# Two-layer graph kernel on one core: h transposed by VectorE blocks and a DRAM scratch in place of TensorE

## The chip, the cores and the metric

The kernel runs on one core of a Trainium2 chip. The metric is the device time of one execution in microseconds (us); lower is better. Engines: PE is TensorE (matrix products), DVE is VectorE, ACT is ScalarE, POOL is GpSimd, SP is SyncE, which here only issues DMAs. Each engine works through its own instructions in order and waits on semaphores.

## The reference, cut to what matters

128 graphs of 128 nodes with 512 features, one adjacency matrix for all, all in fp32:

```python
h = jnp.maximum(_layernorm(x, axis=-1), 0.0)
# layer 0, all products over d, e, m
z_l, z_g, v = h @ W_lang.T, h @ W_grav.T, h @ W_V.T
zn  = z_l / jnp.maximum(norm(z_l), EPS)
A_l = jnp.maximum(zn @ zn.T, 0) * not_eye * adj
A_g = jnp.exp(-squared_distances(z_g) / (2 * sigma * sigma)) * not_eye * adj
K   = w_l * A_l / rowsum(A_l) + (1 - w_l) * A_g / rowsum(A_g)
x   = x + (K @ v) @ W_O.T
h   = jnp.maximum(_layernorm(x, axis=-1), 0.0)
# layer 1: W = adj * adj
x   = x + einsum('bnf,nm->bmf', h, W) + bias
```

## The kernel before, in words

The 128 graphs are worked in 32 groups (NG) of 4 (GB). A semaphore counts everything that is handed on; nothing is planned at run time, the order on each engine is written out by hand in a function `iteration(i)` per engine (PE line 858, ACT line 381, DVE line 644, POOL line 312, SP line 216). Groups 2 to 30 run as a loop, the others are unrolled. A matrix product in fp32 precision is made of three products of fp32r halves: every operand is split into a `hi` part (written by ACT, from PSUM) and a `lo` part (the difference, written by DVE, line 529 for all products from PSUM).

A group i goes through these stages on PE, in this order:

- Y stage: 8 blocks of 3, 6, 9 or 12 products (`y_block`, a over 4, l over 2; 60 products of 512 columns), from the transposed h (`hT`) and weights folded in the setup. ACT writes `y_hi` (line 388), DVE `y_lo` (line 529). Between block 6 and 7 stand 4 transposes of K of the group before (line 837).
- K v stage: 12 products for the group before (`k_v`), whose result DVE adds to x (`residual`, lines 596 and 600: x2 and its statistics).
- P stage: 48 products of 256 columns into `p_ps`; ACT copies them out in two halves (line 410).
- V stage: per graph 12 products of hT with MT (`v_done`), then 4 transposes of h of the NEXT group (`transposes_h`, line 819), 128x128 each, into the same ring of four PSUM banks. ACT writes `v_hi` (line 422) and `hT_hi` (line 378), DVE `v_lo` and `hT_lo` (line 529). After graph 2 stand 8 transposes of P (line 897), which wait for `p_shifted` (ACT line 456).
- Layer 1 stage: 12 products for the group before (`layer1`), from `h2` hi and lo; DVE adds them to x_out (line 642), and SP stores x_out.

A use of a ring bank waits until DVE has drained the use four before it (`free`, line 811). So the first Y block of a group waits for the first x_out of the stage before.

What the change touches besides: the statistics of x of the next group stand on DVE inside the Y stage (`x_stats`, line 541, 4 instructions around `kt_lo`, line 586); POOL makes factors of them (`norm1`, lines 264 to 278), ACT applies them after the Y stage (`apply_norm1`, line 373: h). For layer 1, POOL makes factors of the statistics of x2 (`norm2`, the same lines 264 to 278), ACT writes `h2f` with them (`h2_full`, line 444), ACT copies `h2_hi` (line 451), POOL takes `h2_lo` (line 295). POOL also adds the bias (line 288) and multiplies out the diagonal of P (line 302), of which DVE takes row sums (lines 693, 695) for the shift on ACT (line 456). DVE adds P and its transpose (`sum_s`, line 708), ACT takes the exponential (line 461).

SP per group: load of x of group i+2 (line 200, 1 MB), the row norms out to DRAM and back spread over all partitions (lines 212 and 214), four stores of 256 KB (line 206).

Of the kernel before, what the change touches and what calls it, by code (L numbers as in the profile page):

```python
# [5 lines left out]
ALU = mybir.AluOpType  # L25
# [5 lines left out]
P = 128  # L31
GB = 4
# [6 lines left out]
def gnn_pair(nc, x, adj, w_lang, w_grav, w_v, w_o, gate_logit, log_sigma, bias, out):  # L39
# [9 lines left out]
    blk = {ac: n for n, ac in enumerate(TRI)}  # L49

# [4 lines left out]
    PER = G_USES + GB + 2 * GB + GB  # L55
# [4 lines left out]

    HI_PER = G_USES + 2 * GB

# [6 lines left out]
    with ExitStack() as ctx:  # L69
# [48 lines left out]

        raw_l = x2[:, :, :]
# [10 lines left out]

        rn_dram = nc.dram_tensor("rn_dram", [P, GB], F32).ap()
# [45 lines left out]
        h2_split_dve = sem("h2_split_dve")  # L177
        ln2_last = sem("ln2_last")
# [10 lines left out]
        def wait_for(eng, sem, count):  # L189

            if not isinstance(count, int) or count > 0:
                eng.wait_ge(sem, count)

# [4 lines left out]
        def _(sp):  # L198
# [16 lines left out]

            def iteration(i, load=True, store=True, after=True):
                if load:
# [8 lines left out]
                if store:  # L226
                    store_out(i - 1, first_use(i) + PER - GB * (1 if after else 2))

# [15 lines left out]
            store_out(NG - 1, first_use(NG))  # L244
# [116 lines left out]
        def _(act):  # L361
# [14 lines left out]
            def t_hi(g, b, n):  # L376
                act.wait_ge(t_done, GB * g + b + 1)
                act.activation(hT[0][:, :, b], bank(n).rearrange("p (c m) -> p c m", c=C), ACT.Copy)\
                   .then_inc(hi_ready, 1)

            def iteration(i, before=True, after=True):
# [3 lines left out]
                for a in range(C):  # L385
                    for l in range(2):
# [16 lines left out]
                if after:  # L403
                    apply_norm1(i + 1)
# [13 lines left out]
                for b in range(GB):  # L418
# [5 lines left out]
                    if after:  # L424
                        t_hi(i + 1, b, n)
                        n += 1
# [10 lines left out]
            def h2_full(g, b, last=False):  # L437
# [65 lines left out]
            apply_norm1(0, wait_free=False)  # L503
            lw_hi(1, side, side_hi)
            for b in range(GB):
                t_hi(0, b, SETUP + b)
# [15 lines left out]
        def _(dve):  # L522
# [11 lines left out]
            def x_stats(g, b0, b1):  # L534
# [109 lines left out]
            def iteration(i, before=True, after=True):  # L644
# [36 lines left out]
                for b in range(GB):  # L681
                    hi = hi + 1
                    lo(v[1][:, b], bank(n), v[0][:, b], hi).then_inc(drained, 1)
                    n += 1
                    hi = hi + 1
# [10 lines left out]
                    if b == 2:  # L696
                        sum_s(i)
                if before:
# [95 lines left out]

            iteration(0, before=False)
            iteration(1)
            with dve.Fori(2, NG - 1) as i:
                iteration(i)
            iteration(NG - 1, after=False)
            g = NG - 1  # L800
            residual(g, 0, first_use(g) + PER - GB, last=True)
# [8 lines left out]
        def _(pe):  # L810
# [4 lines left out]
            def transposes_h(g, b, n, use):  # L815
# [153 lines left out]
```

## Time and profile before

| | |
|---|---|
| median of 3 runs | 1308.2 us (1307.92 to 1308.43) |
| span of the profiled execution, first to last instruction | 1305.4 us |
| median of the runs less that span | 2.8 us |
| PE busy | 1281.8 us, 98% |
| DVE busy | 924.4 us, 71% |
| ACT busy | 708.3 us, 54% |
| POOL busy | 610.3 us, 47% |
| mean granted TensorE clock | 0.997 of full speed |
| DMA | 80.02 MB, 61 GB/s over the span |

The profile is of one execution. No time of its own around its span is reported for it, so the runs' median stands for it; the two differ by 2.8 us, launch and end. Busy time counts instructions at work; PE's matmuls are pipelined, so they overlap in the records and a busy PE can still wait a little.

### The profile page before, as it was taken

The numbers are of one execution on the slowest core, as the hardware profiler recorded it, in microseconds if no ns is written. First come the engines' busy times: TensorE is split into PE (matmuls) and PEld (weight loads), VectorE is DVE, ScalarE is ACT, GpSimd is POOL, SyncE is SP. The second block draws the span as 40 slices with busy tenths as digits, with TensorE's granted clock in tenths as the row PEclk, the third lists the DMA queues.
The fourth block names the chain that finished last, engine by engine and source line by source line (L and its number), as shares of the span: only waits on it lengthen the run. The fifth ranks groups of instructions, "written<-read, shape, count | busy, mean of one in ns | idle before, by whom it ended". The sixth has DMA issues, their size and how long they took to land.

```text
span 1305.4 us, 22778 instructions
## 1 busy us (share of the span) xinstructions
PE 1281.8 (98%) x6820; PEld 1094.9 (84%) x6820; DVE 924.4 (71%) x1609; ACT 708.3 (54%) x1324; POOL 610.3 (47%) x995
## 2 busy tenths in 40 slices
PE   7999999999999999999999999999999999999995
PEld 6888888888888888888888888888888888888884
DVE  5477666777666777666778666778666778666678
ACT  5445655545655545655545655545555555555534
POOL 1124555444555444455444455444455444455534
PEclk9999999999999999999999999999999999999998
DMA  5011221111221121221121221121221121221011
GB/s 204 33 31 51 73 70 43 64 68 45 72 72 40 64 72 40 72 72 40 64 72 40 72 72 40 64 72 40 72 72 41 64 71 40 72 72 51 22 41 65
DMA packets 47006, 80.02 MB, mean 61 GB/s; under 512 B 7952, under 2 KB 8080, under 8 KB 46992
## 3 DMA queue, kind: packets, MB, share of 16 engines
q1 hardware_dynamic: 46416, 79.51, 18.3%
q10 hardware_dynamic: 576, 0.33, 0.1%
q8 instruction: 8, 0.13, 0.0%
q14 instruction: 6, 0.05, 0.0%
HBM read 46.20 MB, written 33.62 MB: 61 GB/s over the span
## 4 chain that ended last, share of the span: by engine, by line
PE 95%; DVE 3%; ACT 1%; DMA 1%; issue 0%; POOL 0%; SPq 0%; DVEq 0%
PE ring L824 74%; PE p_ps L824 14%; PE ring L819 4%; PE p_ps L897 2%; PE kt_ps L837 1%; DMA h2f<-in_L_gnn_W_grav 1%; DVE x_out L642 0%; DVE hT_lo L529 0%; ACT h L373 0%; DVE bn L600 0%; DVE y_lo L746 0%; DVE x L596 0%; DVE bn L541 0%; DVE K L580 0%; DVE Lw_lo L761 0%
## 5 line engine op out<-in xcount | busy, mean ns | idle before, releaser
L529 DVE TENSOR_TENSOR v_lo<-ring,v_hi 128x512 fp32r<-128x512 f32 x128 | 88.5, 692 | 290.2 <-ACT v_hi L422 290.2
L388 ACT ACTIVATE y_hi<-ring 128x512 fp32r<-128x512 f32 x256 | 149.0, 594 | 253.1 <-PE ring L824 250.6
L264 POOL TENSOR_TENSOR ln<-bn 128x4 f32<-128x4 f32 x63 | 13.1, 208 | 546.2 <-DVE bn L541 533.1
L824 PE MATMUL ring<-hT_hi,Lw_hi 128*128 128x512 f32 x640 | 252.5, 395 | 3.1 <-DVE hT_lo L529 3.1
L824 PE MATMUL ring<-hT_hi,Lw_lo 128*128 128x512 f32 x640 | 249.7, 390 | 0.0
L824 PE MATMUL ring<-hT_lo,Lw_hi 128*128 128x512 f32 x640 | 249.1, 389 | 0.0
L824 PE MATMUL ring<-MT_hi,hT_hi 128*128 128x512 f32 x512 | 208.7, 408 | 0.0
L824 PE MATMUL ring<-MT_hi,hT_lo 128*128 128x512 f32 x512 | 201.0, 393 | 0.0
L824 PE MATMUL ring<-MT_lo,hT_hi 128*128 128x512 f32 x512 | 200.3, 391 | 0.0
L295 POOL TENSOR_TENSOR h_lo<-h2f,h_hi 128x512 fp32r<-128x512 f32 x124 | 157.9, 1295 | 57.8 <-ACT h_hi L451 57.8
L529 DVE TENSOR_TENSOR y_lo<-ring,y_hi 128x512 fp32r<-128x512 f32 x256 | 170.1, 685 | 13.2 <-ACT y_hi L388 12.8
L288 POOL TENSOR_TENSOR x_out<-x,bias_sb 128x512 f32<-128x512 f32 x128 | 163.4, 1299 | 21.4 <-DVE bn L600 19.6
L824 PE MATMUL p_ps<-y_hi,hT_lo 128*128 128x256 f32 x512 | 144.9, 283 | 0.0
L824 PE MATMUL p_ps<-y_lo,hT_hi 128*128 128x256 f32 x512 | 144.9, 283 | 0.0
L824 PE MATMUL p_ps<-y_hi,hT_hi 128*128 128x256 f32 x512 | 144.7, 283 | 0.0
L824 PEld LDWEIGHTS ring<-hT_hi,Lw_hi 128*128 128x128 f32 x640 | 120.2, 188 | 27.6 <-issue 1.9
L373 ACT ACTIVATE h<-x_ring,ln 128x512 f32 (+1 forms) x128 | 94.0, 807 | 87.9 <-POOL ln L278 87.9
L824 PEld LDWEIGHTS ring<-hT_hi,Lw_lo 128*128 128x128 f32 x640 | 120.1, 188 | 25.7
L824 PEld LDWEIGHTS ring<-hT_lo,Lw_hi 128*128 128x128 f32 x640 | 120.3, 188 | 24.2
L824 PEld LDWEIGHTS ring<-MT_hi,hT_lo 128*128 128x128 f32 x512 | 96.1, 188 | 21.5
L824 PEld LDWEIGHTS ring<-MT_lo,hT_hi 128*128 128x128 f32 x512 | 96.7, 189 | 16.5
L824 PEld LDWEIGHTS ring<-MT_hi,hT_hi 128*128 128x128 f32 x512 | 96.5, 188 | 16.3
(160 smaller groups left out, 2586.0 us busy)
## 6 DMA issues: line engine op xcount, KB each, us to landing
x_ring<-in_x SPq DMA_DIRECT2D x32, 1024.0 KB, 5.3
out<-x_out SPq DMA_DIRECT2D x128, 256.0 KB, 2.1
rn_cols<-rn_dram SPq DMA_DIRECT2D x31, 256.0 KB, 3.6
x<-in_L_gnn_W_lang SPq DMA_DIRECT2D x4, 256.0 KB, 5.5
h2f<-in_L_gnn_W_grav SPq DMA_DIRECT2D x1, 1024.0 KB, 8.9
chain<-in_L_gnn_W_O SPq DMA_DIRECT2D x1, 1024.0 KB, 12.8
x_ring<-in_L_gnn_W_V SPq DMA_DIRECT2D x1, 1024.0 KB, 14.6
rn_dram<-rn SPq DMA_DIRECT2D x31, 2.0 KB, 1.4
```

What stands on the lines that cost most here:

```text
L264: pool.tensor_tensor(t[:, SUM], bn[:, :, 1], bn[:, :, 4], ALU.add).then_inc(step, 1)
L288: pool.tensor_tensor(x_out[:, b], x2[:, b], bias_sb[:, :], ALU.add).then_inc(x2b_ready, 1)
L295: pool.tensor_tensor(h2[1][:, b], h2f[:, b], h2[0][:, b].bitcast(F32), ALU.subtract)\
L373: act.activation(h[:, b], xb, ACT.Relu, bias=ln1[:, SHIFT, b:b + 1], scale=ln1[:, RSTD, b:b + 1]).then_inc(h_ready, 1)
L388: act.activation(y[0][:, a, :, l], bank(n).rearrange("p (b m) -> p b m", b=GB), ACT.Copy)\
L529: return dve.tensor_tensor(out, ps, part(hi), ALU.subtract)
L819: mm = pe.transpose(bank(n)[:, c * P:(c + 1) * P], h[:, b, c * P:(c + 1) * P], ident[:, :])
L824: mm = pe.matmul(out, lhsT, rhs, start=(k == 0), stop=(k == len(terms) - 1))
L837: mm = pe.transpose(kt_ps[:, b], K[:, b], ident[:, :])
L897: mm = pe.transpose(p_ps[:, k // 2, k % 2], P_sb[:, k // 2, k % 2], ident[:, :])
```

## The change

h of the next group is no longer transposed by PE. ACT normalizes h during the last two Y blocks; DVE transposes it in 32x32 blocks (4 instructions of 128x512), into the memory of `h2f`; one DMA writes these blocks to a DRAM scratch (1 MB), four DMAs of 256 KB read them back, each into 32 partitions, so that the blocks land in the rows of the full transpose (`h_turned`); ACT and DVE split `hT` from there instead of from PSUM. Because `h2f` holds the blocks until they are out, `h2_full` waits for `turned`. The statistics of x move to the V stage of the group before. The ring of banks has 4 uses less per group.

```diff
@@ SP
+            def turn_h(g):
+                sp.wait_ge(blocks_ready, GB * g)
+                sp.dma_start(blocks_dram, h_blocks).then_inc(blocks_stored, 16)
+                sp.wait_ge(blocks_stored, 16 * g)
+                for j in range(NQ):
+                    sp.dma_start(h_turned[j * Q:(j + 1) * Q], blocks_dram[:, j].rearrange("(i p) e -> p i e", p=Q))\
+                      .then_inc(turned, 16)
+
             def iteration(i, load=True, store=True, after=True):
+                if after:
+                    turn_h(i + 1)
                 if load:
...
@@ ACT
-            def apply_norm1(g, wait_free=True):
-                act.wait_ge(ln1_step, LN_STEPS * (g + 1))
-                if wait_free:
-                    act.wait_ge(t_done, GB * g)
-                for b in range(GB):
+            def normalize(g, b0):
+                if b0 == 0:
+                    act.wait_ge(ln1_step, LN_STEPS * (g + 1))
...
+                for b in range(b0, b0 + GB // 2):
...
+            def turned_hi(g, b):
+                if b == 0:
+                    act.wait_ge(turned, TURN * g)
+                act.wait_ge(v_done, GB * (g - 1) + b + 1)
+                act.activation(hT_columns(0, b), h_columns(b), ACT.Copy).then_inc(ht_hi, 1)
...
+                        if after and G_USES - 2 <= n < G_USES:
+                            normalize(i + 1, (n - G_USES + 2) * GB // 2)
...
-                if after:
-                    apply_norm1(i + 1)
...
                     if after:
-                        t_hi(i + 1, b, n)
-                        n += 1
+                        turned_hi(i + 1, b)
...
@@ def h2_full
                 if b == 0:
                     wait_for(act, h2_split, GB * g)
+                    act.wait_ge(turned, TURN * (min(g + 2, NG - 1) if isinstance(g, int) else g + 2))
@@ DVE
+            def turn_blocks(g, b):
+                if b == 0 and not (isinstance(g, int) and g < 3):
+                    dve.wait_ge(h2_split, GB * (g - 2))
+                dve.wait_ge(h_ready, GB * g + b + 1)
+                out = h_blocks.rearrange("p j (c b q) -> p c b j q", c=C, b=GB)[:, :, b]
+                dve.transpose(out, h[:, b].rearrange("p (c j q) -> p c j q", c=C, j=NQ)).then_inc(blocks_ready, 1)
+
+            def turned_lo(g, b):
+                dve.wait_ge(ht_hi, GB * (g - 1) + b + 1)
+                dve.tensor_tensor(hT_columns(1, b), h_columns(b), part(hT_columns(0, b)), ALU.subtract)\
+                   .then_inc(ht_lo, 1)
...
-                        if n == G_USES - 2:
-                            if before and after:
-                                x_stats(i + 1, 0, GB // 2)
-                            if before:
-                                kt_lo(i - 1)
-                            if before and after:
-                                x_stats(i + 1, GB // 2, GB)
-                        if not before and n == G_USES:
-                            x_stats(i + 1, 0, GB)
+                        if after and n >= G_USES - 1:
+                            turn_blocks(i + 1, 2 * (n - G_USES + 1))
+                        if before and n == G_USES - 1:
+                            kt_lo(i - 1)
+                        if after and n >= G_USES - 1:
+                            turn_blocks(i + 1, 2 * (n - G_USES + 1) + 1)
...
-                    t_lo(b, n, hi).then_inc(drained, 1 if before or b < GB - 1 else 1 + GB)
-                    n += 1
+                    turned_lo(i + 1, b)
...
                     if b == 2:
                         sum_s(i)
+                    if stats and b >= 2:
+                        x_stats(i + 2, (b - 2) * GB // 2, (b - 1) * GB // 2)
@@ PE, iteration
+                wait_for(pe, ht_lo, GB * i)
...
-                    if after:
-                        transposes_h(i + 1, b, n, use + n)
-                        n += 1
```

Group 0's h is still transposed by PE, in the setup.

## Rows read from the trace of the kernel before

**Rows 1.** Head of the page: busy time per engine.
```profile
PE 1281.8 (98%) x6820; PEld 1094.9 (84%) x6820; DVE 924.4 (71%) x1609; ACT 708.3 (54%) x1324; POOL 610.3 (47%) x995
```

**Rows 2.** Chain that ended last, one group: start us, duration us, what.
```profile
568.53 0.44 PE ring L819 x4
568.97 2.76 PE ring L824 x12
...
579.45 13.65 PE ring L824 x60
...
604.78 2.75 PE ring L824 x12
...
618.45 13.65 PE ring L824 x60
```

**Rows 3.** Timeline of DVE, same group: start, duration, line, operation, count.
```profile
596.98 0.69 DVE L529 TENSOR_TENSOR y_lo<-ring,y_hi 128x512 fp32r<-128x512 f32 x1 [0.21 <-ACT y_hi L388]
597.59 1.28 DVE L596 TENSOR_TENSOR x<-ring,x_ring 128x512 f32<-128x512 f32 x2
601.16 1.28 DVE L600 BATCH_NORM_STATS2 bn<-x 128x6 f32<-128x512 f32 x2
618.68 0.69 DVE L529 TENSOR_TENSOR v_lo<-ring,v_hi 128x512 fp32r<-128x512 f32 x1 [0.94 <-ACT v_hi L422]
619.88 1.88 DVE L642 TENSOR_TENSOR x_out<-ring,x_out 128x512 f32<-128x512 f32 x3
```

**Rows 4.** Timeline of ACT, same group.
```profile
605.78 1.52 ACT L444 ACTIVATE h2f<-x,ln 128x512 f32<-128x512 f32 x2 [0.37 <-POOL ln L278]
607.57 0.60 ACT L422 ACTIVATE v_hi<-ring 128x512 fp32r<-128x512 f32 x1 [0.26 <-PE ring L824]
611.84 0.58 ACT L422 ACTIVATE v_hi<-ring 128x512 fp32r<-128x512 f32 x1
612.79 1.14 ACT L451 ACTIVATE h_hi<-h2f 128x512 fp32r<-128x512 f32 x2
```

**Rows 5.** The page's costliest groups: instructions that the change adds, by their nearest kind.
```profile
L541 DVE BATCH_NORM_STATS2 bn<-x_ring 128x6 f32 x116 | 74.1, 681 | 0.0
L550 DVE TENSOR_TENSOR chain<-chain,rn_cols 128x512 f32<-128x512 f32 x31 | 33.1, 1068 | 0.0
L708 DVE TENSOR_TENSOR chain<-p_ps,chain 128x1024 f32<-128x1024 f32 x32 | 38.9, 1215 | 0.0
```

**Rows 6.** The page's DMA issues: KB each, median us to landing.
```profile
x_ring<-in_x SPq DMA_DIRECT2D x32, 1024.0 KB, 5.3
out<-x_out SPq DMA_DIRECT2D x128, 256.0 KB, 2.1
```

**Rows 7.** Load of x alone, window 600 to 610 us in 40 slices: GB/s.
```profile
GB/s 0 0 0 0 0 0 0 0 0 0 98 147 41 131 229 156 385 393 434 410 426 401 410 336 156 33 8 0 0 0 0 0 0 0 0 0 0 0 0 0
```

**Rows 8.** Start of the kernel: SP issues four loads of 256 KB; ACT starts on each.
```profile
0.81 1.81 SPq L231 DMA_DIRECT2D x<-in_L_gnn_W_lang  x4
...
4.82 0.63 ACT L477 ACTIVATE y_hi<-x 128x512 fp32r<-128x512 f32 x1 [0.85 <-DMA x<-in_L_gnn_W_lang]
...
8.62 0.63 ACT L477 ACTIVATE y_hi<-x 128x512 fp32r<-128x512 f32 x1 [0.57 <-DMA x<-in_L_gnn_W_lang]
```

**Rows 9.** Last group: DVE beside POOL at work.
```profile
1278.33 1.14 DVE L568 TENSOR_TENSOR deg<-deg,rn 128x8 f32<-128x8 f32 x1
1298.53 1.47 DVE L637 TENSOR_TENSOR h_lo<-h2f,h_hi 128x512 fp32r<-128x512 f32 x1
1276.76 2.69 POOL L295 TENSOR_TENSOR h_lo<-h2f,h_hi 128x512 fp32r<-128x512 f32 x2 [2.82 <-ACT h_hi L451]
1296.93 2.52 POOL L288 TENSOR_TENSOR x_out<-x,bias_sb 128x512 f32<-128x512 f32 x2
```

**Rows 10.** SP's issues in the same group.
```profile
601.56 0.41 SPq L200 DMA_DIRECT2D x_ring<-in_x  x1
613.38 0.33 SPq L214 DMA_DIRECT2D rn_cols<-rn_dram  x1
```

More of the change, by code:

```diff
@@ L31 @@
 P = 128
+Q = 32
 GB = 4
@@ L49, in gnn_pair @@
     blk = {ac: n for n, ac in enumerate(TRI)}
+    NQ = P // Q
+    TURN = 16 * NQ
+    assert C == NQ
     G_USES = 2 * C
     SETUP = C
-    PER = G_USES + GB + 2 * GB + GB
+    PER = G_USES + GB + GB + GB
     def first_use(i):
         return SETUP + GB + PER * i
-    HI_PER = G_USES + 2 * GB
+    HI_PER = G_USES + GB
     def first_hi(i):
@@ L116, in gnn_pair @@
         deg = sb("deg", [P, 4, GB, 2])
+        h_turned = sb("h_turned", [P, NQ, C * GB * Q])
+        h_blocks = h2f[:, :, :].rearrange("p b d -> p (b d)").rearrange("p (j e) -> p j e", j=NQ)
         raw_l = x2[:, :, :]
@@ L177, in gnn_pair @@
         h2_split_dve = sem("h2_split_dve")
+        blocks_ready, blocks_stored, turned = sem("blocks_ready"), sem("blocks_stored"), sem("turned")
+        ht_hi, ht_lo = sem("ht_hi"), sem("ht_lo")
         ln2_last = sem("ln2_last")
@@ L192, in wait_for, with h_columns, hT_columns @@
                 eng.wait_ge(sem, count)
+        def h_columns(b):
+            return h_turned[:, :, :].rearrange("p i (c b q) -> p c b i q", c=C, b=GB)[:, :, b]
+        def hT_columns(part, b):
+            return hT[part][:, :, b].rearrange("p c (i q) -> p c i q", q=Q)
         block = ctx.enter_context(nc.Block())
@@ L226, in iteration @@
                 if store:
-                    store_out(i - 1, first_use(i) + PER - GB * (1 if after else 2))
+                    store_out(i - 1, first_use(i) + PER - GB)
             w_rows = w_lang.rearrange("(c p) n -> p c n", p=P)
@@ L365, in _ @@
             act.dma_start(bias_sb[:, :], bias.unsqueeze(0).to_broadcast([P, D])).then_inc(consts_loaded, 16)
-            def apply_norm1(g, wait_free=True):
-                act.wait_ge(ln1_step, LN_STEPS * (g + 1))
-                if wait_free:
-                    act.wait_ge(t_done, GB * g)
-                for b in range(GB):
+            def normalize(g, b0):
+                if b0 == 0:
+                    act.wait_ge(ln1_step, LN_STEPS * (g + 1))
+                    if isinstance(g, int) and g == 1:
+                        act.wait_ge(t_done, GB)
+                    elif not isinstance(g, int) or g > 1:
+                        act.wait_ge(blocks_ready, GB * (g - 1))
+                for b in range(b0, b0 + GB // 2):
                     xb = x_ring[:, bass.ds(g % SLOTS, 1), b].rearrange("p s d -> p (s d)")
@@ L502, in _ @@
             act.activation(sig, lsig, ACT.Exp).then_inc(exp_gate, 1)
-            apply_norm1(0, wait_free=False)
+            normalize(0, 0)
+            normalize(0, GB // 2)
             lw_hi(1, side, side_hi)
             for b in range(GB):
-                t_hi(0, b, SETUP + b)
+                t_hi(b, SETUP + b)
             act.wait_ge(a2_step, 1)
@@ L642, in output, with iteration @@
                 dve.tensor_tensor(x_out[:, b], bank(n), x_out[:, b], ALU.add).then_inc(drained, 1)
-            def iteration(i, before=True, after=True):
+            def iteration(i, before=True, after=True, stats=True):
                 n = 0
@@ L682, in iteration @@
                     hi = hi + 1
-                    lo(v[1][:, b], bank(n), v[0][:, b], hi).then_inc(drained, 1)
+                    lo(v[1][:, b], bank(n), v[0][:, b], hi)\
+                        .then_inc(drained, 1 if before or b < GB - 1 else 1 + GB)
                     n += 1
-                    hi = hi + 1
-                    t_lo(b, n, hi).then_inc(drained, 1 if before or b < GB - 1 else 1 + GB)
-                    n += 1
+                    turned_lo(i + 1, b)
                     if b == 0:
@@ L793, in _ @@
             dve.tensor_tensor(A2[1][:, :], adj2[:, :], part(A2[0][:, :]), ALU.subtract).then_inc(a2_step, 1)
+            x_stats(1, 0, GB)
             iteration(0, before=False)
             iteration(1)
-            with dve.Fori(2, NG - 1) as i:
+            with dve.Fori(2, NG - 2) as i:
                 iteration(i)
+            iteration(NG - 2, stats=False)
             iteration(NG - 1, after=False)
             g = NG - 1
-            residual(g, 0, first_use(g) + PER - GB, last=True)
+            residual(g, 0, first_use(NG), last=True)
             h2_lo(g, 0)
@@ L813, in free, with transposes_h @@
                 wait_for(pe, drained, use - BANKS + 1)
-            def transposes_h(g, b, n, use):
-                pe.wait_ge(h_ready, GB * g + b + 1)
+            def transposes_h(b, n, use):
+                pe.wait_ge(h_ready, b + 1)
                 free(use)
@@ L922, in _ @@
             for b in range(GB):
[L923 removed]
+                transposes_h(b, SETUP + b, SETUP + b)
             pe.wait_ge(w_loaded["o"], 16)
@@ L938, in _ @@
             g = NG - 1
-            use = first_use(g) + PER - GB
+            use = first_use(NG)
             pe.wait_ge(kt_split, NG)
```

8 lines of the change are left out of this document (4 added, 4 removed).

## The prediction

> **What bounds the kernel now.** I read the head of the page first: PE is busy 98% of the span, the next engine, DVE, 71% [rows 1]. Then the chain that ended last, around one group in the middle: it runs on PE alone, stage behind stage, with no wait between [rows 2]. Its long pieces of 13.65 us (12 products of layer 1, then 48 of the next Y stage) start at 579.45 and 618.45, so a group takes 39.00 us, and 30 of them are alike. 12 of 60 products into that piece, at 618.45 + 2.7 = 621.1, the next Y stage starts. Last I read the timelines of DVE, ACT and SP over the same group [rows 3, 4, 10], to see how far behind PE they run. Here the cover is thin. The first Y block needs the bank that the first x_out frees; that x_out starts at 619.88 and ends at 620.56 [rows 3], only 0.5 us ahead of 621.1. ACT starts h2f 0.37 us after POOL's factors are there, and v_hi 0.26 us after PE's result [rows 4]. So PE bounds, but one queue of dependences (x2 statistics, POOL's factors, h2f, v_hi, v_lo, x_out) is under a microsecond from bounding too.
>
> **The change, part by part.**
>
> 1. PE loses the transposes of h: 4 x 0.44 us per group [rows 2], 1.76 us, in 31 groups 55 us. This is a gain only as long as PE sets the end.
>
> 2. DVE gets 4 block transposes of 128x512 per group. The trace has none. The nearest row is bn_stats over 128x512 from SBUF at 0.68 us [rows 5]; in a row such instructions start 0.60 apart (two take 1.28 us [rows 3]). Above it I bound by the slowest 128x512 there is, 1.07 us, which reads with a stride [rows 5]; below by nothing, since a gain is excluded. I take 0.60, because one pass over 512 elements costs the same in all other DVE rows. The four x statistics leave this place, so DVE's work in the Y stage is the same, but its place is not: the statistics stood ahead of the last y_lo, and DVE even waited 0.21 us for ACT there [rows 3]. Transposes 2 and 3 stand behind it, since ACT normalizes them only in block 7, and so ahead of the residual: this starts at 597.59 + 1.2 = 598.8 in place of 597.59. x2's statistics, norm2 and h2f follow 1.2 us later: 605.78 becomes 607.0.
>
> 3. The way through DRAM. The last blocks are ready at 597.59 + 2 x 0.60 + 0.08 = 598.9. SP's queue is clear: it has stored the group before and waits here (the load of x started at 601.56 [rows 10] and now goes behind the turn; its data is wanted only some 10 us later; the row norms come later still and have slack too). Out: 1 MB to DRAM. A store of 256 KB lands in 2.1 us [rows 6]; the 0.79 MB more, at the load's full pace of about 0.4 MB per us [rows 7], cost 2.0: 4.1 us. The upper bound is x's load of 1 MB, 5.3 [rows 6]. I take 4.1, as the direction is that of the store. Back: four DMAs of 256 KB, issued in a row. Lower bound: the single load of 1 MB, about 5.4 us. Upper: at half its pace. Its data take 1.05 MB / 0.4 = 2.6 us at full pace [rows 7], so half adds 2.6: 8.0. Between stands the nearest row in form, four loads of 256 KB issued one behind the other: from 0.81 to 8.62, 7.8 us, landing after the first about 1.3 us apart [rows 8] (in the start-up of the kernel, beside small loads). I take 7.8. The blocks are back at 598.9 + 4.1 + 7.8 = 610.8.
>
> Each quarter writes only 32 partitions. The Trainium skill (SBUF — State Buffer, Door 1: The DMA port swizzle) says that a transfer into partitions 0 to 31 or 0 to 63 reaches 8 of 16 ports and so about half the bandwidth, and that issuing two such transfers doesn't help. No row here has such a transfer. By that rule the way back takes the 8.0 above and the total is 6 us higher; by the row of x's load it takes 5.4, the second rival.
>
> 4. The new wait on ACT. h2f waits for `turned`: 610.8, not 605.78, nor the 607.0 of part 2. Queued behind it on ACT are v_hi, hT_hi, the rest of h2f, the shift, h2_hi. From h2f to v_hi of graph 1 ACT takes 611.84 - 605.78 = 6.06, less the 0.26 wait: 5.80; from there to v_hi of graph 2 it takes 2.05 (h2_hi starts at 612.79 and takes 1.14 [rows 4]). So v_hi 2 starts at 618.65 and ends at 619.25. On the way PE waits: its transposes of P need the shift, done at 616.6, while PE, without the transposes of h, comes there at 604.78 + 3 x 2.76 = 613.1 [rows 2]. That stall of 3.5 us is not extra; it lies beside the same path.
>
> 5. DVE behind v_hi 2, all in order: v_lo 0.60, hT_lo 0.60, the sum with P transposed 1.2 [rows 5], two x statistics 1.2, v_lo 0.60, hT_lo 0.60, two x statistics 1.2, x_out 0.68. Together 6.68. The x statistics are the 2.4 us that the change moves here; before, x_out came straight behind hT_lo. x_out ends at 625.95.
>
> 6. A collision. hT_lo read PSUM and SBUF; now it reads SBUF twice. In the last group, DVE instructions that read SBUF twice stretch where POOL is at work: a 128x8 one takes 1.14 us, ending as POOL's h_lo does, and h_lo on DVE takes 1.47 in place of 0.68, by what POOL's bias addition had left [rows 9]. POOL's h_lo of 4 x 1.26 us starts at 618.3 in the new order, so hT_lo 2 at 619.9 falls into the second of them, ending at 620.8: 0.8 us. Bounds: nothing, and twice 1.26. The Trainium skill (SBUF — State Buffer, SBUF: two separate sides) calls this port pair an exclusive lock against a DVE instruction with two SBUF inputs; by that rule the 0.8 stands, and without it, the total is 24 us lower.
>
> **Sum.** x_out ends at 626.75, 5.65 us after the 621.1 at which the Y stage starts now: a group takes 44.65 us. 30 groups (1 to 30) have the wait: 30 x 5.65 = 169.5. Group 0 has no h2f, its blocks are back long before the V stage: 1 us less. Group 30 has no x statistics: some 2 us less. Span 1305.4 + 169.5 - 3 = 1471.9; with the 2.8 us by which the runs' median lies over the span, 1474.7.
>
> **Rivals.**
>
> *A, full pace on the way back.* The quarters stream like one load: 5.4 us. Then h2f starts at 608.4, a group costs 3.25 more, 30 x 3.25 - 3 + 1308.2 = 1403 us. For it: the same packets of 2 KB; against: rows 8 and four separate issues. 20%.
>
> *B, the way through DRAM is covered.* It decides where the round trip is under 607.0 - 598.9 = 8.1 us; then only parts 2, 5 and 6 are left: 5.65 - 3.8 = 1.85 per group, 1361 us; without the collision 1337. Against it: a store and a load of 1 MB alone take 4.1 + 5.4 = 9.5. 6%.
>
> *C, PE goes on setting the end: faster.* If x_out still ends ahead of PE, all of part 1 is gained: 31 x 1.76 = 55, 1254 us. The place is x_out behind DVE's queue in the V stage. It decides if h2f starts no later than about 605, that is if the turn's wait never ends last, and DVE's statistics run in its gaps. For it: DVE is idle for several us in every V stage, and PE is the only engine over 71% [rows 1]. Against it: those gaps lie before v_hi 0, not behind v_hi 2, where 6.68 us stand in a row. 8%.
>
> *D, everything at its upper end.* Out 5.3, back 8.0, DVE transposes 1.07 (0.8 more), a second collision: 8 to 8.5 us per group, about 1550 us. 6%.
>
> That the change does nothing is no case: 1.8 us of PE work and a round trip per group cannot vanish together by chance; 1% for no change, where gain and wait balance. That PE gets slower by clock is not one either: it was granted full speed throughout and is still busy over 80%.
>
> **How the numbers follow.** Forecast, 59%: 1475 us. Its own spread, by collision and start-up share of rows 8, is 1440 to 1510. To leave out no more than 2 in 10, the range goes down through rival A to 1385 and up part of the way to D, 1520; B, C and the end of D are left out. Slower by over 0.2% (about what a measurement of this kernel can tell from no change) are the forecast, A, B and D: 91%. Within 0.2%: 1%. Faster: C, 8%.
>
> **What the profile of after would show.** Right: a period of 44 to 45 us; PE busy near 84%, with idle time before the transposes of P and before the first Y block; ACT's largest wait in the middle groups at h2f, ended by the DMA into h_turned; out in about 4 us, back in about 8; a DVE transpose of 0.7 us; hT_lo with a mean over 0.68. Wrong: the chain still on PE alone (C); ACT's h2f ended by POOL's factors (B); quarters that land in under 4 us each with a return under 6 in all (A); or the chain going through POOL or the load of x, which no part here expects.

## The result, and the profile after

The changed kernel takes 1467.2 us (median of 4 runs, 1465.9 to 1468.2) against 1308.1 us before: ratio 1.1218, 95% interval 1.1202 to 1.1234, so 159 us slower, inside the range and 8 us under the forecast. The profiled execution took 1465.9 us with a span of 1464.2. One execution further below, of the kernel with no trip, ran at a mean clock of 0.557, took 2063 us and is left out.

Head of the page of the changed kernel, its chain by engine and line, and its DMA issues (KB each, median us to landing):

```profile
PE 1269.1 (87%) x6324; PEld 1043.1 (71%) x6324; DVE 1020.8 (70%) x1733; ACT 701.8 (48%) x1324; POOL 651.9 (45%) x995
...
PE 38%; DMA 19%; DVE 16%; ACT 11%; issue 11%; SPq 2%; DVEq 1%; ACTq 0%; POOL 0%
...
x_ring<-in_x SPq DMA_DIRECT2D x32, 1024.0 KB, 7.8
...
blocks_dram<-h2f SPq DMA_DIRECT2D x31, 1024.0 KB, 3.9
h_turned<-blocks_dram SPq DMA_DIRECT2D x124, 256.0 KB, 5.1
```

[rows 1] showed PE at 98%. Now PE is at 87% with 496 instructions less, and the chain, PE alone around the group of [rows 2], is more than half on others, 19% of it on the two transfers. Three views of one group show it in order of time. The timeline of SP (start, duration, line, what):

```profile
623.34 0.33 SPq L215 DMA_DIRECT2D blocks_dram<-h2f  x1
627.22 1.75 SPq L218 DMA_DIRECT2D h_turned<-blocks_dram  x4
629.46 0.42 SPq L197 DMA_DIRECT2D x_ring<-in_x  x1
...
667.69 0.33 SPq L215 DMA_DIRECT2D blocks_dram<-h2f  x1
```

The timelines of ACT and, below it, DVE, for the same group; they answer to [rows 3, 4]:

```profile
634.74 1.52 ACT L460 ACTIVATE h2f<-x,ln 128x512 f32<-128x512 f32 x2 [4.90 <-DMA h_turned<-blocks_dram]
...
642.45 0.58 ACT L438 ACTIVATE v_hi<-ring 128x512 fp32r<-128x512 f32 x1
```

```profile
622.01 1.29 DVE L565 STREAM_TRANSPOSE h2f<-h 128x512 f32<-128x512 f32 x2
...
643.68 1.59 DVE L569 TENSOR_TENSOR hT_lo<-h_turned,hT_hi 128x512 fp32r<-128x512 f32 x1
645.19 1.21 DVE L734 TENSOR_TENSOR chain<-p_ps,chain 128x1024 f32<-128x1024 f32 x1
646.33 1.27 DVE L558 BATCH_NORM_STATS2 bn<-x_ring 128x6 f32 x2
647.52 0.67 DVE L546 TENSOR_TENSOR v_lo<-ring,v_hi 128x512 fp32r<-128x512 f32 x1
648.11 0.67 DVE L569 TENSOR_TENSOR hT_lo<-h_turned,hT_hi 128x512 fp32r<-128x512 f32 x1
648.71 1.27 DVE L558 BATCH_NORM_STATS2 bn<-x_ring 128x6 f32 x2
649.91 1.86 DVE L671 TENSOR_TENSOR x_out<-ring,x_out 128x512 f32<-128x512 f32 x3
```

POOL's h_lo, beside which the hT_lo of 1.59 us runs:

```profile
642.11 5.55 POOL L302 TENSOR_TENSOR h_lo<-h2f,h_hi 128x512 fp32r<-128x512 f32 x4 [1.34 <-ACT h_hi L467]
```

How to read them together: the blocks leave at 623.34 and are in DRAM at 627.22 (the return is issued then); ACT starts h2f at 634.74, 7.5 us later, after 4.90 us of waiting for the DMA; v_hi of graph 2 ends at 643.03; from there DVE works without a gap to x_out. PE's timeline shows what all this holds up, the first products of the transposes of P, of layer 1 (twice) and of the next Y stage, with the waits before them:

```profile
640.56 1.09 PE L925 MATMUL p_ps<-ident,chain 128*128 128x128 f32 x8 [3.17 <-ACT chain L472]
...
646.55 0.49 PE L852 MATMUL ring<-h_hi,A_hi 128*128 128x512 f32 x1 [0.74 <-POOL h_lo L302]
...
648.24 0.50 PE L852 MATMUL ring<-h_hi,A_hi 128*128 128x512 f32 x1 [0.74 <-DVE v_lo L546]
...
650.63 0.50 PE L852 MATMUL ring<-hT_hi,Lw_hi 128*128 128x512 f32 x1 [1.42 <-DVE x_out L671]
```

The period, from one issue of the blocks to the next, is 667.69 - 623.34 = 44.35 us, where it was 39.00. From here on "period" is read in this way, from SP's timeline.

### The profile page after: what moved, and what is told of

Same layout as the page of the kernel before. It is cut to its first block, busy times and chain, and to the rows that moved or that the text cites. A ratio compares the mean times of both kernels' runs of the same rounds, so it can differ in the third digit from the quotient of the medians.

```text
span 1464.2 us, 21983 instructions
## 1 busy us (share of the span) xinstructions
PE 1269.1 (87%) x6324; PEld 1043.1 (71%) x6324; DVE 1020.8 (70%) x1733; ACT 701.8 (48%) x1324; POOL 651.9 (45%) x995
## 4 chain that ended last, share of the span: by engine, by line
PE 38%; DMA 19%; DVE 16%; ACT 11%; issue 11%; SPq 2%; DVEq 1%; ACTq 0%; POOL 0%
PE ring L852 35%; DMA h_turned<-blocks_dram 11%; DMA blocks_dram<-h2f 7%; DVE bn L558 5%; ACT v_hi L438 3%; DVE sq L717 3%; SPq L218 2%; DVE hT_lo L569 2%; PE p_ps L852 2%; ACT h_hi L467 2%; ACT chain L472 2%; ACT h2f L460 2%; DVE h2f L565 2%; DVE x_out L671 1%; DVE chain L734 1%
## 5 line engine op out<-in xcount | busy, mean ns | idle before, releaser
L852 PE MATMUL ring<-hT_hi,Lw_hi 128*128 128x512 f32 x640 | 257.1, 402 | 43.5 <-DVE x_out L671 40.1
L302 POOL TENSOR_TENSOR h_lo<-h2f,h_hi 128x512 fp32r<-128x512 f32 x124 | 171.8, 1414 | 45.3 <-ACT h_hi L467 45.3
L460 ACT ACTIVATE h2f<-x,ln 128x512 f32<-128x512 f32 x128 | 97.2, 805 | 156.2 <-DMA h_turned<-blocks_dram 147.2
L426 ACT ACTIVATE chain<-p_ps 128x512 f32<-128x512 f32 x64 | 38.3, 598 | 230.2 <-PE p_ps L852 230.2
L925 PE MATMUL p_ps<-ident,chain 128*128 128x128 f32 x256 | 38.4, 298 | 96.0 <-ACT chain L472 96.0
```

What stands on the lines that cost most here:

```text
L302: pool.tensor_tensor(h2[1][:, b], h2f[:, b], h2[0][:, b].bitcast(F32), ALU.subtract)\
L426: act.activation(P_sb[:, 2 * half:2 * half + 2], p_ps[:, 2 * half:2 * half + 2], ACT.Copy)\
L852: mm = pe.matmul(out, lhsT, rhs, start=(k == 0), stop=(k == len(terms) - 1))
L925: mm = pe.transpose(p_ps[:, k // 2, k % 2], P_sb[:, k // 2, k % 2], ident[:, :])
```

## The experiments

The forecast was right in time. But each of its terms could be wrong with another making up for it, so I took them apart one by one: the x statistics behind v_hi (2.4 us), h2f's wait for the blocks (3.8 us), and the form of the trip. The collision of hT_lo with POOL was not taken out by itself. A second question came up on the way: can the change be made to pay?

**x statistics out of the tail.**

```diff
-                    if stats and b >= 2:
-                        x_stats(i + 2, (b - 2) * GB // 2, (b - 1) * GB // 2)
+                    if stats and b < 2:
+                        x_stats(i + 2, b * GB // 2, (b + 1) * GB // 2)
```

> The changed kernel with the statistics of x in the V stage behind graphs 0 and 1 in place of graphs 2 and 3. My theory: v_lo of graph 2 to the first x_out is a row of DVE instructions that sets the end, and the 2.4 us of statistics stand in it. In front of it DVE idles 1.62 and 0.76 us behind graphs 0 and 1, so the first pair costs nothing and the second about 0.4: 2.0 us less per group, 44.35 becomes 42.4, the total 1467 - 60 = 1407 us. Rival, that only the wait for the way through DRAM decides: DVE's work behind it would be covered by PE, no change, 1467 us.

Measured: 1415.6 us, 52 less, where the expectation had 60. Period 42.6 us (43.4 in two groups): 1.8 of the 2.4 us come out. The rival (no change) is refuted: the statistics are a term of their own, and most of it was real. The mean clock is 0.968 here in place of 0.986. The windows show its falls to half around the transposes of P (at 662 to 668 us and the like), where PE has slack: groups with a fall of some 3 us take as long as groups without one, and in the two groups of 43.4 us it lasts some 7 us.

**The same statistics late in the kernel before**, which says whether they cost by themselves:

```diff
                         if n == G_USES - 2:
-                            if before and after:
-                                x_stats(i + 1, 0, GB // 2)
                             if before:
                                 kt_lo(i - 1)
-                            if before and after:
-                                x_stats(i + 1, GB // 2, GB)
...
                     if b == 2:
                         sum_s(i)
+                    if stats and b >= 2:
+                        x_stats(i + 2, (b - 2) * GB // 2, (b - 1) * GB // 2)
```

> The kernel before, with nothing changed but the place of the statistics of x: in the V stage behind graphs 2 and 3, as the change has them. My theory: DVE has 0.94 us free ahead of v_lo 3, the rest of the 2.4 us stands ahead of the first x_out, which then ends 1.46 us later, at 622.0 in place of 620.56, 0.9 behind PE: 30 x 0.9 = 27, 1335 us. Rival, that PE covers it: 1308 us.

Measured: 1339.1 us, ratio 1.0237 (1.0220 to 1.0254), period 40.1 us; the theory had 1335. So 1.1 of the 2.4 us end behind PE even with no transposes, no trip and no new wait: the cover of 0.5 us between x_out and the Y block that the prediction read in [rows 3] was as thin as it looked.

**Blocks in memory of their own**, so that h2f need not wait (diag and A are free at that time):

```diff
-        h_blocks = h2f[:, :, :]...
+        h_blocks = chain[:, 1:3]...
...
             def diagonal(g):
+                pool.wait_ge(blocks_stored, 16 * (g + 1))
...
-                    act.wait_ge(turned, ...)
...
             def turn_blocks(g, b):
-                    dve.wait_ge(h2_split, GB * (g - 2))
+                    dve.wait_ge(k_ready, g - 1)
...
```

> The changed kernel with the 32x32 blocks in the memory of diag and A (free at that time) in place of h2f's, so that h2f does not wait for the blocks' return; hT_hi of graph 0 still does, and ACT stands there. My theory: h2f starts 3.3 us earlier, at POOL's factors, but hT_hi 0 waits where it stood 2 us later before; what follows on ACT moves up by 2.0 us: 42.4 us per group, 1407 us. Rival, that the shared buffer is the whole price of the wait: 3.3 us per group, 1367 us.

Measured: 1466.8 us. A miss by 60 us: no gain at all. The timeline of ACT shows that the edit did what it should: h2f starts behind POOL's factors, 8.05 us after the blocks were issued (at 625.62) in place of 11.40, and it is hT_hi that waits for the DMA, until 11.42 us after the issue; in the changed kernel it stood at 13.31. So ACT gains the 2 us that were foreseen.

```profile
633.67 1.52 ACT L460 ACTIVATE h2f<-x,ln 128x512 f32<-128x512 f32 x2 [1.54 <-POOL ln L285]
635.10 0.58 ACT L439 ACTIVATE v_hi<-ring 128x512 fp32r<-128x512 f32 x1
637.04 0.63 ACT L396 ACTIVATE hT_hi<-h_turned 128x512 fp32r<-128x512 f32 x1 [1.37 <-DMA h_turned<-blocks_dram]
```

Of the timelines of POOL and DVE in the same group, one line each:

```profile
636.04 2.54 POOL L295 TENSOR_TENSOR x_out<-x,bias_sb 128x512 f32<-128x512 f32 x2
...
637.71 1.43 DVE L569 TENSOR_TENSOR hT_lo<-h_turned,hT_hi 128x512 fp32r<-128x512 f32 x1 [1.31 <-ACT hT_hi L396]
```

Two things took the gain. hT_lo 0 now runs beside POOL's bias addition and takes 1.43 us in place of 0.68. And the clock, which the windows of 2 us at the start of the Y stage show (busy time per engine and number of instructions, then granted clock, DMA share, GB/s):

```profile
648.00:650.00 2.00, 1.25 (x6) 0.61 (x4) 2.00 (x5) 0.23 (x1) 0.72 (x1) 1.00 0.00 0
650.00:652.00 2.00, 0.58 (x3) 0.31 (x2) 2.00 (x4) 0.00 (x0) 0.72 (x4) 0.82 0.00 0
652.00:654.00 2.00, 2.00 (x6) 1.52 (x6) 2.00 (x4) 0.60 (x1) 1.76 (x5) 0.50 0.68 253
654.00:656.00 2.00, 2.00 (x9) 1.65 (x8) 2.00 (x4) 0.60 (x1) 1.22 (x2) 0.83 0.65 245
```

The granted clock goes from full (2.4 GHz) to half (1.2 GHz) for some 3 us, and the products of the next Y stage come 0.43 us apart in place of 0.23. PE had idled 1.95 us before the transposes of P and 0.73, 0.75 and 1.42 us shortly before the fall. The fall comes in most groups, not in all: the periods are 44.4 to 44.7, and every eighth is 43.1. So a fall costs 1.5 us, and without it the edit would be worth 1.2 us per group.

**The same with PE kept busy.** 14 products whose results nobody uses, on operands that lie ready, stand where PE would idle; nothing else differs.

```diff
+                        if before and after:
+                            filler(6)
                         pe.wait_ge(p_shifted, i + 1)
...
+                        if after and b >= 2:
+                            filler(2)
                         layer1(i - 1, b, n + b, use + n + b)
+                    if after:
+                        filler(4)
```

> The run with own blocks, and on PE 14 products per group (128x512, one pass each, result used by nobody) put in front of its waits: 6 before the transposes of P, 2 before each of the last two products of layer 1, 4 before the Y stage. In the run with own blocks the first 6 products of the Y stage ran at 0.43 us each in place of 0.23, the granted clock 0.50 there. My theory: the clock fell because PE had stood still before; filled, it stays at 1.00, the Y stage gets 1.3 us back and so do the blocks: 43.1 us per group, 1428 us. Rival, that the fall has another reason or costs nothing on the path: 1467 us or more.

Measured: 1428.9 us, mean clock 0.998 in place of 0.954, and a period of 43.0 to 43.2 in every group but the first. That is the time foreseen. It shows that the 38 us were the clock's, and that PE's idleness brought its fall about. The Trainium skill (TensorE: Matmul & The Clock Gate, Why this matters for your kernels) warns of idle gaps between bursts of products. Here no gap before the fall was longer than 1.95 us, while the changed kernel, with one of 3.17 us at the same place, shows no fall in the group above.

**The form of the way back.** First one DMA of 1 MB into 128 partitions in place of four quarters:

```diff
-                for j in range(NQ):
-                    sp.dma_start(h_turned[j * Q:(j + 1) * Q], blocks_dram[:, j]...)
+                sp.dma_start(h_turned[:, :, :], blocks_dram).then_inc(turned, 16)
```

> The changed kernel with the return in one DMA of 1 MB into all 128 partitions in place of four of 256 KB into 32 each; the same bytes, but the blocks are not put in their places, so h of later groups is not transposed as a whole. My theory (32 partitions at a time take it to half pace): the return takes 5.4 us as x's load of before in place of 7.4, so 2.0 less per group, 1407 us. Rival, the time lies in reading what was just written to DRAM: 7.4 us again, 1467 us.

Then four DMAs of 256 KB again, each into 128 partitions:

```diff
-                    sp.dma_start(h_turned[j * Q:(j + 1) * Q], blocks_dram[:, j]...)
+                    sp.dma_start(h_turned[:, j], blocks_dram[:, j]).then_inc(turned, 16)
```

> As the run with one return, but in four DMAs of 256 KB, each into all 128 partitions (one quarter of the columns each); the same bytes and packets of 2 KB, the blocks again not put in their places. It parts the number of issues from the number of partitions. My theory: partitions decide, and this run is within 0.5 us per group of the one return: 5.4 to 5.9 us, 1407 to 1422 us. Rival, four issues in a row decide: 7.4 us as in the changed kernel, 1467 us.

Measured: 1413.5 us for the single return (1407 foreseen) and 1469.0 us for the four wide ones, where the theory had 1407 to 1422 and the rival 1467. On its time alone the second would be the rival's; the traces say otherwise. The DMA issues of the two pages (one return; four wide ones):

```profile
h_turned<-blocks_dram SPq DMA_DIRECT2D x31, 1024.0 KB, 4.8
```

```profile
h_turned<-blocks_dram SPq DMA_DIRECT2D x124, 256.0 KB, 3.7
```

A quarter lands in 5.1 us when it goes to 32 partitions and in 3.7 when it goes to 128. So the form of the destination costs 1.4 to 1.7 us of the way back (h2f waits 3.2 us on average in place of 4.9: 96 in place of 147 us over 30 groups), and four issues in a row of 0.4 us each cost another 1.0 against a single one, with which h2f waits 2.2. This agrees with the Trainium skill (SBUF — State Buffer, Door 1) in direction; half the pace, as the prediction estimated it, would have made it 2.6 us. But the time of the four wide returns did not fall: their mean clock is 0.960, the windows show a fall at the start of the Y stage in every group but the first, and the periods are 44.3 to 44.6 from the third group on. If the fall costs the 1.5 us that it costs above, an estimate, they would be 42.9 without it. The single return alternates. Its issues of the blocks, three periods:

```profile
562.41 0.33 SPq L215 DMA_DIRECT2D blocks_dram<-h2f  x1
...
604.23 0.33 SPq L215 DMA_DIRECT2D blocks_dram<-h2f  x1
...
646.04 0.33 SPq L215 DMA_DIRECT2D blocks_dram<-h2f  x1
...
689.40 0.33 SPq L215 DMA_DIRECT2D blocks_dram<-h2f  x1
```

41.8, 41.8 and 43.4 us: over the whole run 41.8 and 43.3 for the most part turn about, and the 13 groups of 43.3 are those in which the clock falls.

**No trip at all.** DVE writes the blocks straight into `h_turned`; no DMA, no wait for one.

```diff
-                if after:
-                    turn_h(i + 1)
...
-h_blocks = h2f...
+h_blocks = h_turned[:, :, :]
```

> The changed kernel without the way through DRAM: VectorE transposes its 32x32 blocks straight into h_turned and both DMA steps are left out, so h of later groups is turned in blocks only. Everything else stays, the late statistics and the shifted residual too. My theory: h2f starts at POOL's factors, 3.35 us earlier; hT_lo of graph 0 then meets POOL's bias addition (0.75 us, as in the run with own blocks) and, if PE's clock falls as it did there, 1.3 us go as well. 44.35 - 3.35 + 0.75 = 41.75 us per group, 1389 us; with the clock's fall 43.05, 1428 us. Rival, that the way through DRAM is the whole loss: 1308 us or less, since PE has 1.76 us less to do per group.

Measured: 1410.8 us, in one execution. The theory had 1389 without a fall of the clock and 1428 with one in every group; the rival (1308 or less) is refuted. The periods are 41.8 and 43.3 for the most part turn about, the same as with a single return, and again the 13 groups of 43.3 are those with a fall, some 20 us in all. That is the bound behind the trip: with the trip gone, the kernel still takes 103 us more than before. The timeline of DVE in one group:

```profile
654.21 1.49 DVE L564 TENSOR_TENSOR hT_lo<-h_turned,hT_hi 128x512 fp32r<-128x512 f32 x1
...
661.30 1.60 DVE L564 TENSOR_TENSOR hT_lo<-h_turned,hT_hi 128x512 fp32r<-128x512 f32 x1
...
663.96 1.27 DVE L555 BATCH_NORM_STATS2 bn<-x_ring 128x6 f32 x2
...
666.34 1.27 DVE L555 BATCH_NORM_STATS2 bn<-x_ring 128x6 f32 x2
```

Two collisions of 0.8 and 0.9 us, the 2.4 us of statistics, and h2f 1.2 us late behind transposes 2 and 3: these are matters of order, not of the trip. That they can be put right is for the next kernels to show.

**The order put right.** If the cost lies in places, the change can be kept and the places mended. The first attempt: own blocks, `h_turned` on the memory of h, four slots of x with the load one group earlier, the x statistics behind the residual, where DVE waits for v_hi, and the copies out of the turned h put off by one or two graphs.

```diff
-    SLOTS = 3
+    SLOTS = 4
...
                 n += GB
+                if after and stats:
+                    x_stats(i + 2, 0, GB)
...
-                    turned_lo(i + 1, b)
+                    if b == 1:
+                        turned_lo(i + 1, 0)
+                        turned_lo(i + 1, 1)
+                    if b == 3:
+                        turned_lo(i + 1, 3)
...
                         sum_s(i)
+                        turned_lo(i + 1, 2)
...
```

> The whole change in another order, complete: blocks in the memory of diag and A; h_turned in the memory of h, which frees the room for a fourth slot of x; so x is loaded a group earlier and its statistics stand in DVE's long gap behind the residual; hT_hi and hT_lo of graphs 0 and 1 come behind h2_hi 0 and 1, the others behind. The blocks land 28.4 us into the group and are wanted at about 30.6, so nothing waits for them. My theory: the queue behind v_hi 2 is v_lo, sum, hT_lo, v_lo, hT_lo, x_out, and the first x_out ends at 37.5 to 38.4 us into the group, against PE's 37.2: 38.2 us per group, 30 x 0.8 less than before, 1284 us. Rival: collisions of hT_lo with POOL's h_lo (up to 1.26 each, three of them) and a fall of PE's clock (1.3) eat this: 39.5 to 41 us per group, 1325 to 1370 us.

Measured: 1342.7 us (1339.4 to 1344.7), 58 above the theory; the rival was right. Period 39.7 us, and 41.3 in the seven groups in which the clock falls, some 11 us in all. Timeline of DVE in the V stage:

```profile
625.44 1.03 DVE L733 TENSOR_SCALAR sqc<-sq 128x4 f32<-128x4 f32 x1
...
628.79 2.57 DVE L577 TENSOR_TENSOR hT_lo<-h,hT_hi 128x512 fp32r<-128x512 f32 x2 [0.87 <-ACT hT_hi L399]
...
633.01 1.30 DVE L577 TENSOR_TENSOR hT_lo<-h,hT_hi 128x512 fp32r<-128x512 f32 x1
```

Alone these take 0.17, 1.28 and 0.68 us: 2.8 us lost beside POOL. And h2f still comes late: it waits 1.6 us for POOL's factors. With these durations I wrote the queues of the five engines out as a timetable (for each instruction its pitch, what it waits for, and a lock between DVE instructions with two SBUF inputs and POOL's large ones) and tried the places of the copies in it. The best order has normalization after the fourth and sixth y copy, all transposes after the sixth y, the first two copies ahead of the shift:

```diff
+                        if after and n in (4, 6):
+                            normalize(i + 1, (n - 4) * GB // 4)
...
+                        if n == G_USES - 2:
+                            if after:
+                                turn_blocks(i + 1, 0)
+                                turn_blocks(i + 1, 1)
+                            if before:
+                                kt_lo(i - 1)
+                            if after:
+                                turn_blocks(i + 1, 2)
+                                turn_blocks(i + 1, 3)
...
+                    if after and b == 0:
+                        turned_hi(i + 1, 0)
+                        turned_hi(i + 1, 1)
                         shift(i, 1)
...
+                        turned_lo(i + 1, 0)
+                        turned_lo(i + 1, 1)
                     if b == 2:
                         sum_s(i)
+                        turned_lo(i + 1, 3)
...
```

> The re-ordered change once more, with every step of the turned h moved a few microseconds earlier: ScalarE normalizes the next group's h behind the fourth and the sixth y product instead of the sixth and the seventh, VectorE turns all four blocks behind the sixth y and before the last two (they stood behind the seventh and eighth), hT_hi 0 and 1 come in the slot of graph 0 before the shift, hT_lo 0 and 1 behind sqc, and hT_lo 3 behind the sum. In the run before this one the period was 39.7 us with collisions of VectorE's subtractions with GpSimd's additions (hT_lo 0 and 1 2.57 us for two, hT_lo 2 1.30, sqc 1.03 in place of 0.17). My theory: the cost of the change is a matter of order alone, the 11.3 us of the DRAM trip is covered when the blocks leave at the sixth y, and the 1.76 us of transposes that TensorE is rid of show at last: my timetable of the queues gives 38.1 us per group where it gives 38.9 for the kernel before (measured 39.0), so 1308.1 less 30 x 0.8 = 1284 us, 1275 to 1300. Rival: VectorE and GpSimd meet wherever the copies are put, because VectorE's third of the group is full: then the collisions cost what TensorE gains, and the time is 1305 to 1345. Second rival: the four normalizations ahead of the last y copies hold the y banks back, TensorE waits in the Y stage, its granted clock falls under 0.98 and the time lies over 1345.

Measured: **1282.1 us** (1281.0 to 1282.9), ratio 0.9805 (0.9788 to 0.9821), the fastest of all: 26 us under the kernel before. The head of the page, the chain by engine, and SP's issues of two groups:

```profile
PE 1234.4 (96%) x6324; PEld 1045.0 (82%) x6324; DVE 1032.7 (81%) x1733; ACT 708.9 (55%) x1324; POOL 671.8 (53%) x995
...
PE 74%; DVE 12%; ACT 7%; issue 6%; DMA 1%; ACTq 0%; POOL 0%; DVEq 0%; SPq 0%
```

```profile
624.33 0.33 SPq L215 DMA_DIRECT2D blocks_dram<-chain  x1
628.22 1.75 SPq L218 DMA_DIRECT2D h<-blocks_dram  x4
...
662.35 0.33 SPq L215 DMA_DIRECT2D blocks_dram<-chain  x1
```

The period is 38.0 to 38.1 us in every group but the first (38.02 here; the timetable said 38.1), the trip takes as long as ever (3.9 us out), and no engine waits for it: DMA is 1% of the chain. PE gets 0.98 of its 1.76 us; 0.65 of the rest is a wait for x_out before the last product of layer 1:

```profile
647.37 0.49 PE L866 MATMUL ring<-h_hi,A_hi 128*128 128x512 f32 x1 [0.65 <-DVE x_out L678]
```

Order alone could hardly have brought the kernel before there: its PE is busy 40.00 of 40 us in the middle of the run. That was not tried.

**Which part of the order it was.** Two kernels, each the 1282.1 us one with one thing put back. In the first, normalization and transposes stand where the change has them:

```diff
-                        if after and n in (4, 6):
-                            normalize(i + 1, (n - 4) * GB // 4)
+                        if after and G_USES - 2 <= n < G_USES:
+                            normalize(i + 1, (n - G_USES + 2) * GB // 2)
...
-                        if n == G_USES - 2:
-                            if after:
-                                turn_blocks(i + 1, 0)
...
+                        if after and n >= G_USES - 1:
+                            turn_blocks(i + 1, 2 * (n - G_USES + 1))
...
```

> The kernel of 1282.1 us with one thing put back: normalization and block transposes stand where the change has them (behind the sixth and seventh y copy and the seventh and eighth y), so that the blocks leave later; the x statistics, the memories and the places of the copies out of the turned h stay. My theory: the trip through DRAM is then uncovered by the time by which the blocks leave later (about 1.2 us); my timetable gives 39.3 us per group against 38.1, so 1282 + 30 x 1.2 = 1318 us, 1300 to 1335. Rival: the places of the copies alone made the gain over the 1342.7 us of the first re-ordered kernel, and 1.2 us of lateness are swallowed by the slack before the first hT_hi: 1280 to 1295.

Measured: 1296.3 us (1294.4 to 1297.0), period 38.5 to 38.7. That lies between the ranges of the theory (1300 to 1335) and the rival (1280 to 1295), nearer to the rival, and the timetable's 39.3 us was a miss: the trip stays covered, and no engine waits for it. What is lost is h2f again, behind the residual that stands behind transposes 2 and 3. Its waits in the two kernels, in this one and in the 1282.1 us one:

```profile
ACT h2f L467 <- POOL ln L288: 46.4, 30, 1.6
```

```profile
ACT h2f L467 <- POOL ln L288: 10.9, 30, 0.4
```

1.2 us per group. So of the 61 us between the two re-ordered kernels 46 belong to the places of the copies (some 11 of them by the falls of the clock, which this kernel does not have) and 14 to the earlier blocks.

In the second, the x statistics are back in the V stage:

```diff
-                if after and stats:
-                    x_stats(i + 2, 0, GB)
...
+                    if stats and b >= 2:
+                        x_stats(i + 2, (b - 2) * GB // 2, (b - 1) * GB // 2)
```

> The kernel of 1282.1 us with one other thing put back: the four bn_stats on the next x stand behind the v_lo of graphs 2 and 3, as the change has them, and not behind the residual, where VectorE waits 3.4 us for v_hi anyway. My theory: they stand between the last v_lo and x_out, for which TensorE waits, so their 2.4 us come out nearly whole unless VectorE waits there: my timetable gives 39.8 us per group against 38.1, so 1282 + 30 x 1.8 = 1335 us, 1320 to 1350, in line with the 51.7 us that the same move gave back in the changed kernel. Rival: VectorE has 0.7 and 0.8 us of waiting before the v_lo of graphs 1 and 2 and little behind them, the statistics fill it, and the kernel stays under 1310.

Measured: 1367.5 us, worse than the 1335 foreseen and than its rival. The period is 39.75 us in every fifth group, 1.73 more, as the timetable had it, and 41.3 in the others, in which the clock falls:

```profile
608.00:610.00 2.00, 0.96 (x3) 0.48 (x3) 2.00 (x5) 0.00 (x0) 0.13 (x1) 1.00 0.00 0
610.00:612.00 2.00, 1.39 (x3) 1.16 (x4) 2.00 (x4) 0.00 (x0) 1.63 (x8) 0.60 0.20 76
612.00:614.00 2.00, 2.00 (x6) 1.53 (x5) 2.00 (x4) 1.02 (x2) 1.86 (x2) 0.55 0.85 318
```

The timetable knew nothing of the clock. The 85 us over the 1282.1 are 29 groups of 1.73 us for the work and, on average, 1.2 for the clock.

## Why the prediction was right, point by point

**Part 1, PE's 1.76 us:** right as work. In the changed kernel nothing of it is seen, since PE waits; only in the 1282.1 us kernel does it come out, by half.

**Part 2, transposes:** right. 0.60 apart (two take 1.29 us), 0.69 each, and transposes 2 and 3 do push the residual and h2f by 1.2 us; the kernel with late blocks shows that term alone, at 0.5 us of the period where PE has other slack.

**Part 3, the trip:** the form was right, both terms a little too high. Out 3.9 us (4.1 taken), back 7.5 (7.8), 11.4 in all against 11.9. The four start-up loads of [rows 8] were the right row: with x's load as the model it would have been 5.4. Rival A, which part 3 calls the second rival, is refuted by 5.1 us for a quarter. What the prediction left out: x's own load stands behind the returns and lands in 7.8 us in place of 5.3 [rows 6]; nobody waits for it.

**Part 4, the wait of h2f:** seen as predicted, ended by the DMA in 30 groups. From h2f to v_hi 2 the text had 7.85 us, the timeline 642.45 - 634.74 = 7.71. PE's stall at the transposes of P is 3.2 us on average (3.5 said).

**Parts 5 and 6, DVE's row and the collision:** from the end of v_hi 2 to the end of the first x_out 7.5 us were summed; measured 650.59 - 643.03 = 7.56. The collision costs 0.9 us (1.59 in place of 0.68) in the instruction named, where 0.8 was taken.

**The sum:** 44.65 us per group against 44.35; 30 x 0.3 = 9 us is the difference in the result. PE's busy share is 87% and not "near 84%". I had taken the 55 us off its busy time and forgot how it is recorded: products overlap (0.39 us long, 0.23 apart), so each wait uncovers a tail of 0.16, and the first product behind a wait takes 0.1 us longer (0.49 or 0.50). In the group shown PE is busy 44.35 us less its four waits, that is 38.28, where 39.00 - 1.76 = 37.24 would be 84%; the rest comes where the clock was low.

**What was right by luck.** Two arguments did not hold up, though the number did. First, the terms do not add up as the text has them. It sums the wait of h2f (3.8 us) and the row behind it (1.85), as if each came back when it is removed. Removing the wait gives 1.2 us (44.35 to 43.1, with PE kept busy), removing the whole trip 2.5 (to 41.8), removing the statistics alone 1.8. Rival B, the trip covered, was priced at 1361 us, and the kernel with no trip takes 1411, some 1391 without its falls of the clock: a second path stands close behind, from POOL's factors through an hT_lo that now collides too (1.49 us). Second, "that PE gets slower by clock is not one either": in the changed kernel itself that held for 25 of the 30 groups of the profile (mean clock 0.986), but the reason given, busy over 80%, is none. With the blocks in their own memory PE is busy 89% and the clock falls in most groups.

Rival C, faster, did not come about in this order, but its place and condition were right: x_out behind DVE's queue, and statistics in DVE's gaps. Set up so, and with other memories for the blocks, the same change gives 1282 us, about half of the gain that C had priced (1254).

**What stays open.** Why the clock falls in one group and not in the next is not settled. The changed kernel idles 0.74, 0.74 and 1.42 us at the same places as the one with its own blocks, and more before, and keeps its full clock in 25 of 30 groups; its falls lie around the transposes of P, where they cost 0.2 us of a period or nothing. In its three other executions the mean clock was 0.963 to 0.982, and they took only 1 to 2 us longer, so the falls differ from one execution to the next as well; in the kernel without a trip the clock falls in some 13 of 30 groups that are alike. Filling the gaps prevents it; more was not tried.

## What to carry to other kernels

A transpose moved off a full engine paid here only once every queue that takes it over had a new order: the same change was 12% slower or 2% faster by the places of a dozen instructions, with the memory of two buffers changed and a fourth slot of x. Write the queues out as a timetable with measured pitches, waits and port collisions before moving work: it forecast 38.1 and 39.8 us for periods of 38.02 and 39.75, but also 39.3 for one of 38.6, and it did not see the clock fall. And when a removed wait brings nothing, look at the granted clock in short windows before doubting the wait.

## What the runs showed of the hardware

- TensorE's granted clock fell to half for about 3 us after short idle gaps (0.73, 0.75, 1.42 us) and cost 1.5 us where that was the start of the Y stage, but nothing that shows in the period where it was around the transposes of P (a few falls there of some 7 us cost 0.2 to 0.9); with products of no use in the gaps it stayed at 0.998 on average, and the kernel was 38 us faster for doing more.
- A VectorE subtraction with two SBUF inputs takes 1.3 to 1.6 us in place of 0.68 beside GpSimd's 128x512 additions and subtractions, and even the small 128x4 tensor_scalar with one input took 0.66 to 1.08 us in place of 0.17 in the re-ordered kernels, where it falls beside GpSimd's bias addition.
- In these kernels 1 MB goes out to DRAM in 3.9 us in one DMA and comes back in 4.8 in one DMA over 128 partitions, or 7.5 in four over 32 partitions each.
- A VectorE transpose of 128x512 float32 in 32x32 blocks takes 0.69 us, where the other 128x512 instructions of VectorE mostly take 0.67 to 0.69 (a strided one 1.07).
